# One product and a square root for the norm's variance, weight splits moved behind VectorE's, and w1 and w2 of three blocks in three rounded passes

## The reference, cut to what matters

```python
xn = _layernorm(x)                                    # (x - m) / sqrt(v + 1e-5), over 128 values
x = x + attn0(xn) + ffn0(xn)
# attn0: in_w, a causal convolution of 4 taps, silu, xp_w, a scan over time, out_w
# ffn0:  h = silu((xn @ w1.T) * s1) * ((xn @ w2.T) * s2)      # 128 -> 512
#        h = gelu((h @ h1.T) * t1); h = gelu((h @ h2.T) * t2)  # 512 -> 512, twice
#        h @ w3.T * s3                                        # 512 -> 128
xn = _layernorm(x)
x = x + ttt(xn) + moe(xn)                             # layer 1: test-time training, mixture of experts
```

## Time and profile before

| | |
|---|---|
| median of 3 runs | 646.53 us (643.77 to 649.48) |
| the profiled execution, its own time | 649.79 us |
| its span, first to last instruction | 647.9 us |
| TensorE busy / VectorE / ScalarE / GpSimd | 590.3 / 474.3 / 300.1 / 287.5 us |
| mean granted TensorE clock | 0.955 of 2.4 GHz |

### The profile page before, as it was taken

The page is one execution under the profiler, slowest core; times in us unless marked ns, Lnnn a source line. Parts: engine busy times, 40 slices in busy tenths (PEclk is TensorE's granted clock), DMA queues, the critical chain, the costliest instruction groups (busy, mean ns, idle before and its releaser), DMA issues.

```text
span 647.9 us, 14287 instructions
## 1 busy us (share of the span) xinstructions
PE 590.3 (91%) x5563; PEld 431.5 (67%) x5563; DVE 474.3 (73%) x898; ACT 300.1 (46%) x582; POOL 287.5 (44%) x267
## 2 busy tenths in 40 slices
PE   3979999999998997997999999899999989988786
PEld 1456676575566654665678778778778768766575
DVE  0593385794696287989769869787869769779892
ACT  1434245544545451633556355556356365344202
POOL 1970000025255353547431855962745945526411
PEclk9999899999897998997999999999999789999789
DMA  7999100001000100002625206234214322100401
GB/s 244 310 298 300 44 1 1 16 6 46 1 0 29 39 16 23 18 2 82 195 69 150 88 8 192 77 101 147 72 35 121 111 91 74 42 19 15 131 17 50
DMA packets 37890, 53.15 MB, mean 82 GB/s; under 512 B 10168, under 2 KB 23120, under 8 KB 37440
## 3 DMA queue, kind: packets, MB, share of 16 engines
q1 hardware_dynamic: 35552, 47.56, 24.4%
q0 software_dynamic: 2272, 4.69, 2.2%
HBM read 36.33 MB, written 15.90 MB: 81 GB/s over the span
## 4 chain that ended last, share of the span: by engine, by line
PE 64%; DVE 24%; POOL 6%; issue 4%; ACT 2%; DMA 0%; POOLq 0%; SPq 0%; ACTq 0%; DVEq 0%
PE ps L984 9%; PE ps L1087 7%; PE ps L841 7%; PE ps L1050 5%; PE ps L1058 4%; PE ps L1153 4%; PE ps L1095 4%; PE ps L847 3%; PE ps L1010 3%; POOL small L693 3%; PE ps L1137 3%; DVE small L1861 2%; PE ps L955 2%; PE ps L901 2%; PE ps L904 2%
## 5 line engine op out<-in xcount | busy, mean ns | idle before, releaser
L693 POOL TENSOR_TENSOR small<-small 128x8 f32<-128x8 f32 x32 | 53.4, 1680 | 108.7 <-DVE small L1799 108.6
L776 POOL TENSOR_TENSOR small<-small 128x8 f32<-128x8 f32 x32 | 51.9, 1635 | 37.8 <-DVE small L1791 37.8
L634 POOL TENSOR_TENSOR small<-small 128x4 f32<-128x4 f32 x8 | 8.7, 1093 | 116.7 <-DVE small L1554 116.7
L737 POOL DMA_INDIRECT ys_dram<-ybuf,slot_row x39 | 51.7, 1324 | 12.9 <-issue 8.6
L1407 ACT ACTIVATE sq<-ps 128x512 f32<-128x512 f32 x32 | 19.1, 597 | 72.0 <-PE ps L1087 72.0
L1439 ACT ACTIVATE work<-ps,b1t 128x128 f32<-128x128 f32 x156 | 44.5, 368 | 15.8 <-PE ps L1050 14.9
L1137 PE MATMUL ps<-grad,l 64*64 64x64 f32 x1024 | 33.0, 231 | 11.6 <-DVE grad L1876 10.8
L1398 ACT ACTIVATE x_query<-ps 128x512 f32<-128x512 f32 x32 | 17.5, 595 | 54.6 <-PE ps L1010 54.6
L1137 PEld LDWEIGHTS ps<-grad,l 64*64 64x64 f32 x1024 | 31.0, 144 | 16.0 <-issue 13.3
L1095 PE MATMUL ps<-grad,mats 64*64 64x512 f32 x224 | 35.7, 682 | 5.7 <-DVE sq L1805 3.4
L841 PE MATMUL ps<-act_parts,h_parts 128*128 128x512 f32 x128 | 37.4, 447 | 3.8 <-DVE act_parts L1721 3.8
(11 more groups left out here) (255 smaller groups left out, 1535.3 us busy)
## 6 DMA issues: line engine op xcount, KB each, us to landing
wtile<-in_mw SPq DMA_DIRECT2D x48, 256.0 KB, 3.4
xs_dram<-ybuf SPq DMA_DIRECT2D x1, 8840.0 KB, 37.8
got<-in_mw SPq DMA_DIRECT2D x30, 256.0 KB
xg<-xs_dram SPq DMA_DIRECT2D x40, 65.0 KB
got<-ys_dram SPq DMA_DIRECT2D x4, 512.0 KB, 5.4
x_sb<-in_xT SPq DMA_DIRECT2D x4, 256.0 KB, 4.8
acc<-in_h SPq DMA_DIRECT2D x1, 1024.0 KB, 6.6
got<-in_h SPq DMA_DIRECT2D x1, 1024.0 KB, 8.7
```

The costliest lines, as they stand in the source:

```text
L693: pool.tensor_tensor(small[:, 240 + 8 * p:248 + 8 * p], small[:, 224 + 8 * p:232 + 8 * p], small[:, 384:392], ALU.pow).then_inc(q_r.sem, 1)
L737: pool.indirect_dma_start(ys_dram, bass.IndirectOffsetOnAxis(ap=slot_row[:, k:k + 1], axis=0), ybuf[:, k // 4 % 2, k % 4], None).then_inc( ...
L776: pool.tensor_tensor(small[:, 16 + 8 * p:24 + 8 * p], small[:, 8 * p:8 * p + 8], small[:, 384:392], ALU.pow).then_inc(z_r.sem, 1)
```

## The change

- **Norm.** The four narrow products are one product of the mean matrix with all 512 columns of squares, so that every partition gets every variance at once. ScalarE takes the root with the epsilon as bias, VectorE takes the reciprocal of the 128x512 result in place and multiplies. `deviations`, `spreads`, `diagonals` and `spread_over` are gone. For `ahead_of[0]`, root, reciprocal and multiplication stand earlier: ScalarE's root ahead of the `h1` gelus, VectorE's part between the two halves of the convolution.
- **w1 and w2.** In blocks 1 to 3 each of the 8 float32 products is three rounded passes. VectorE splits the normalised block into `xn_hi` and `xn_lo` after the rests of `h1`'s activations, GpSimd splits `w1` and `w2`.
- **GpSimd.** The splits of `w1` and `w2` and the four operations for layer 1 wait until VectorE has split block 1 (`x_lo`). The splits of `wk` and `wq` wait until VectorE's last rest of block 3 (`a_gl`), and `split_tokens(0)`, which stood among block 2's work, follows them.

```diff
             def squares_mean(turn, i):
...
-                for j in range(NB // P):
-                    mm = pe.matmul(to[:, j:j + 1], lsq[:, j * P:(j + 1) * P], mats[:, M_MEAN * P:M_MEAN * P + 1],
-                                   start=True, stop=True)
-                mm.then_inc(ln_var, 1)
-            def spread_over(turn, i):
-                pe.wait_ge(ln_dg, norm_no[turn, i] + 1)
-                pe.matmul(slot_bank("norm", turn, i), mat(M_MEAN), lsq, start=True, stop=True).then_inc(ln_bc, 1)
+                pe.matmul(to, mat(M_MEAN), lsq, start=True, stop=True).then_inc(ln_var, 1)
...
+                if i:
+                    pe.wait_ge(x_lo, i)
+                    pe.wait_ge(h_sp, 4 * KC + 4)
                 for m in range(KC):
-                    pe.matmul(open_slot("w1", i, m), w1[:, m * P:(m + 1) * P], xn[:, blk(i)], start=True, stop=True)
-                    pe.matmul(open_slot("w2", i, m), w2[:, m * P:(m + 1) * P], xn[:, blk(i)],
-                              start=True, stop=True).then_inc(a_w12.sem, 1)
+                    for kind, w, parts in (("w1", w1, xb_s), ("w2", w2, xb_t)):
+                        to = open_slot(kind, i, m)
+                        at = slice(m * P, (m + 1) * P)
+                        if i:
+                            pe.matmul(to, parts[:, 0, at], xn_hi[:, :], start=True, stop=False)
+                            pe.matmul(to, parts[:, 1, at], xn_hi[:, :], start=False, stop=False)
+                            mm = pe.matmul(to, parts[:, 0, at], xn_lo[:, :], start=False, stop=True)
+                        else:
+                            mm = pe.matmul(to, w[:, at], xn[:, blk(i)], start=True, stop=True)
+                    mm.then_inc(a_w12.sem, 1)
...
             def spread_in(turn, i):
-                act.wait_ge(ln_bc, n + 1)
-                act.activation(lsq, slot_bank("norm", turn, i), ACT.Copy).then_inc(ln_rb, 1)
+                act.wait_ge(ln_var, n + 1)
+                act.activation(lsq, slot_bank("norm", turn, i), ACT.Sqrt, bias=eps_ln[:, 0:1]).then_inc(ln_rb, 1)
...
             def normalised(turn, i):
+                dve.reciprocal(lsq, lsq).then_inc(ln_iv, 1)
+                dve.wait_ge(ln_iv, n + 1)
...
-                        if m == 1 and t == 1:
-                            diagonals(*ahead_of[0])
                     if m == 0:
-                        deviations(*ahead_of[0])
+                        normalised(*ahead_of[0])
...
-                normalised(*ahead_of[0])
+                if i < NBLK - 1:
+                    dve.wait_ge(ln_out.sem, ln_out.at(norm_no[ahead_of[0]], 1))
+                    dve.tensor_copy(xn_hi[:, :], xn[:, blk(i + 1)]).then_inc(x_hi, 1)
+                    dve.wait_ge(x_hi, i + 1)
+                    tt(xn_lo[:, :], xn[:, blk(i + 1)], xn_hi[:, :], ALU.subtract).then_inc(x_lo, 1)
...
+            pool.wait_ge(x_lo, 1)
+            for w, to in ((w1, xb_s), (w2, xb_t)):
+                pool.tensor_copy(to[:, 0], w).then_inc(h_sp, 1)
+                parts[0] += 2
+                pool.wait_ge(h_sp, parts[0] - 1)
+                pool.tensor_tensor(to[:, 1], w, to[:, 0], ALU.subtract).then_inc(h_sp, 1)
             step(pool.tensor_tensor(wv_f, wk_f, wv_f, ALU.subtract))
...
             pool.wait_ge(ln_out.sem, ln_out.at(norm_no[1, 0], 1))
-            split_tokens(0)
-            spreads(1, 2)
             pool.wait_ge(a_h1.sem, a_h1.at(NBLK - 1, KC))
+            pool.wait_ge(a_gl.sem, a_gl.at(NBLK - 1, KC))
             split(wk, wk_f)
             split(wq, wq_f)
+            pool.wait_ge(a_w12.sem, a_w12.at(NBLK - 1, KC))
+            split_tokens(0)
```

More of the change, by code:

```diff
@@ L143, in build @@
         xb_t = sb("xb_t", [P, 2, NB], F32R)
+        with ExitStack() as first_layer:
+            xn_hi = first_layer.enter_context(nc.sbuf_tensor("xn_hi", [P, NB], F32R))
         x_less = sb("x_less", [P, NB])
+        xn_lo = sb("xn_lo", [P, NB], F32R)
         work = sb("work", [P, 8192])
@@ L260, in build @@
         eps_set, pads_set = sem("eps_set"), sem("pads_set")
-        ln_centred, ln_sq, ln_var, ln_sd, ln_rs, ln_dg, ln_bc, ln_rb = (
-            sem(n) for n in ("ln_centred", "ln_sq", "ln_var", "ln_sd", "ln_rs", "ln_dg", "ln_bc", "ln_rb"))
+        ln_centred, ln_sq, ln_var, ln_rb, ln_iv = (
+            sem(n) for n in ("ln_centred", "ln_sq", "ln_var", "ln_rb", "ln_iv"))
         ln_out = signal("ln_out", 1)
@@ L274, in build @@
         a_gh, a_gl = signal("a_gh", KC), signal("a_gl", KC)
-        h_sp = sem("h_sp")
+        h_sp, x_hi, x_lo = sem("h_sp"), sem("x_hi"), sem("x_lo")
         a_h1 = signal("a_h1", KC)
@@ L629, in _ @@
             pool.memset(zeros, 0.0).then_inc(zeroed, 1)
[L631 to L634, removed]
             parts = [0]
@@ L893, in _ @@
             squares_mean(0, 0)
-            spread_over(0, 0)
             for i in range(NBLK):
@@ L923, in _ @@
                 by_lo(to, h1_hi, a_h1.sem)
-                spread_over(*ahead_of[0])
                 to = [open_slot("h2", i, m) for m in range(KC)]
@@ L956, in _ @@
                 mm.then_inc(a_w3.sem, 1)
-                if len(ahead_of) == 2:
-                    spread_over(*ahead_of[1])
                 to = open_slot("out", i, 0)
@@ L1184, in _ @@
             key_bias(0, 0)
-            spread_over(1, NBLK - 1)
             keys_through(0, 0)
@@ L1303, in _ @@
             act.wait_ge(eps_set, 3)
-            act.activation(small[:, 100:102], eps_ln, ACT.Square)
+            act.activation(small[:, 100:102], eps_ln, ACT.Sqrt)
             squared(0, 0)
@@ L1328, in _ @@
                     gates_in(i - 2)
+                spread_in(*ahead_of[0])
                 for m in range(KC):
@@ L1333, in _ @@
                                    scale=col("h1_s", m)).then_inc(a_g1.sem, 1)
-                spread_in(*ahead_of[0])
                 for m in range(DC):
@@ L1550, in _ @@
             tt, ts, stt = dve.tensor_tensor, dve.tensor_scalar, dve.scalar_tensor_tensor
-            def deviations(turn, i):
-                dve.wait_ge(ln_var, norm_no[turn, i] + 1)
-                ts(dev[:, 0:4], slot_bank("norm", turn, i)[:, 0:4], LN_EPS, None, ALU.add).then_inc(ln_sd, 1)
-            def diagonals(turn, i):
-                dve.wait_ge(ln_rs, norm_no[turn, i] + 1)
-                for j in range(NB // P):
-                    ins = ts(lsq[:, j * P:(j + 1) * P], mat(M_IDENT), dev[:, j:j + 1], float(P), ALU.mult, ALU.mult)
-                ins.then_inc(ln_dg, 1)
             def normalised(turn, i):
-                dve.wait_ge(ln_rb, norm_no[turn, i] + 1)
+                n = norm_no[turn, i]
+                dve.wait_ge(ln_rb, n + 1)
+                dve.reciprocal(lsq, lsq).then_inc(ln_iv, 1)
+                dve.wait_ge(ln_iv, n + 1)
                 o = xn[:, blk(i)]
@@ L1686, in _ @@
             dve.wait_ge(ld_x, 32)
-            deviations(0, 0)
-            diagonals(0, 0)
             normalised(0, 0)
@@ L1745, in _ @@
                                            ALU.mult, ALU.add).then_inc(a_y.sem, 1)
-                if len(ahead_of) == 2:
-                    deviations(*ahead_of[1])
-                    diagonals(*ahead_of[1])
                 if i == NBLK - 1:
@@ L1768, in _ @@
                         tt(wt[:, 1, half], slot_bank("wt", 0, p), wt[:, 0, half], ALU.subtract).then_inc(w_t, 1)
-            deviations(1, NBLK - 1)
-            diagonals(1, NBLK - 1)
             normalised(1, NBLK - 1)
```

7 lines of the change are left out of this document (1 added, 6 removed).

## The result

The changed kernel takes **657.18 us** in the median of four executions (655.96 to 659.45), the kernel before 646.35 in the runs beside it (643.77 to 649.48): a ratio of **1.017, 95% interval 1.0115 to 1.0224**, slower. The prediction said 650.9, within 633 to 658, and gave "slower" 28%. The measured time lies inside the whole range but outside the forecast's own range, 644 to 655: the range holds because its upper end was kept for a reciprocal of 4.4 us, which did not occur. In the medians the change costs 10.8 us, and the sum gave 4.4. Comparisons leave out executions that stand over 1.5% above the fastest of the same kernel.

What follows compares the result with a forecast made beforehand. Stages were taken as bound by TensorE unless a row shows it waiting. Terms -0.7 - 2.0 - 0.5 + 1.5 + 1.1 + 1.45 + 3.5 = +4.4 us, on a median of 646.5, gave 650.9 us, range 633 to 658.

Steps and rivals of the forecast that it cites:

- forecast's own range: Range of the main forecast, 644 to 655 us, given 47%; the whole range took in a fast and a slow reciprocal.
- the reciprocal: VectorE's 128x512 reciprocal in each norm: 3.4 us, with 0.7 and 4.4 kept as the ends.
- Six places on the path: The reciprocal lies on TensorE's way at the start, in blocks 0 to 3 and at the last norm.
- The first rival: The 128x512 reciprocal is an ordinary instruction of 0.7 us, giving 634.5 us; chance 25%.
- second rival: The reciprocal takes over 8 ns for each element, 4.4 us, giving 657.5 us; chance 16%.
- where the waits stand: TensorE waits about 1.7, 2.7, 4.6 and 4.6 us before h2 in blocks 0 to 3; GpSimd delays block 0's scan.
- Rival three: GpSimd's long row blocks nobody: scan instructions pass beside it, giving 641.4 us; chance 8%.
- TensorE should keep its clock: Block 0: GpSimd's operations no longer lie beside h2, so its 16 passes take 3.80 us instead of 5.49.
- two losses of 1.7 outside what is hidden: Waits of 4.6, 4.6 and 5.5 us in blocks 2 and 3 cost two unhidden clock losses, +3.5 us.
- clock term: The sum's part for low clock behind TensorE's new waits: +3.5 us, between 0 and 5.1.
- 0.7 us gained at the start: Start to in_w: one product, root, reciprocal and multiplication end at 16.3 where in_w started at 17.04, -0.7 us.
- block 0's -2.0: Block 0: h2 starts earlier, but the scan, held by GpSimd, ends at 62.0; -2.0 us with 2.7 of waiting.

Runs made afterwards that it cites:

- e1: Changed kernel without the 128x512 reciprocal in each of the eight norms: mean 634.1 us of the lower pair of executions.
- e2: Changed kernel with every reciprocal of a norm done twice in a row: mean 676.2 us of the lower pair of executions.
- e4: Changed kernel with products nobody reads put into TensorE's waits before h2 in blocks 0 to 3: 660.4 us, against 660.6 by the ratio for the changed kernel.
- e5: Changed kernel with GpSimd's work back where it stood before, new norm and rounded passes kept: 664.4 us, ratio 1.0278 to the kernel before.
- e11: Kernel before with only GpSimd's work in the change's places, w1 and w2 still float32: 649.5 us, ratio 1.0062.
- e3: Changed kernel with the norm as before, rounded passes of w1 and w2 and GpSimd's new order kept: 655.9 us, ratio 1.006 to the kernel before.
- e8: e3 with GpSimd's four operations behind block 0's scan and the tokens' parts ahead of the wk and wq splits: 637.9 us, ratio 0.987 to the kernel before.
- e12: Kernel before with only the new norm, GpSimd's order and float32 w1 and w2 kept: 656.7 us, ratio 1.016.

## Why the prediction came out as it did

| up to | forecast, us against before | measured |
|---|---|---|
| `in_w` of block 0 | -0.7 | 16.56 - 17.04 = -0.5 |
| `h2` of block 0 | -3.0 | 42.97 - 46.14 = -3.2 |
| block 1 | -2.7 | 70.5 - 70.4 = +0.1 |
| block 2 | -3.2 | 115.3 - 114.2 = +1.1 |
| block 3 | -1.7, and 1.7 of clock: 0 | 166.5 - 162.3 = +4.2 |
| layer 1 | -0.6, and 3.5 of clock: +2.9 | 219.2 - 213.7 = +5.5 |
| gates of the last norm | +4.4 | 234.14 - 226.60 = +7.5 |

**Right: the reciprocal.** 3.35 us for 3.4. Six places on the path, in their sum shown by e1 and e2. The first rival (0.7 us) and the second (4.4) are both out. That the measured 657.2 falls on the second rival's 657.5 is chance. The Trainium skill ("VectorE: DVE Perf Modes", First, the fixed hardware budget) names a repeat count of 8; read as eight cycles it gave 4.3 us by estimate, and the row, 3346 ns, decides against that reading.

**Right: where the waits stand.** 2.34, 4.04 and 4.15 before `h2` for 2.7, 4.6 and 4.6; `out_w` behind the scan and GpSimd (62.49 for 62.0); the mask behind GpSimd, 45.8 us behind its block's `in_w` for 47.6. Two sizes are off: 3.48 us before block 0's `h2` for 1.7, since TensorE was ready at 39.5 and not at 41.4, and 2.44 before the mask for the 5.5 that 209.8 - 204.3 gives. Rival three, that GpSimd blocks nobody, is out by the rows of the scan.

**The step that failed: the clock.** "TensorE should keep its clock" in block 0, and "two losses of 1.7 outside what is hidden". With (1 - clock) x length the windows give 1.6 + 1.8 + 0 + 5.1 + 0 = 8.5 us lost before and 3.2 + 3.6 + 2.0 + 4.7 + 1.6 = 15.2 after: +6.7, where the forecast had 3.5 - 1.7 = +1.8. Block 0's `h2` still waited 3.48 us and still took 5.5, which the wait before `out_w` hid; the products behind its scan took 3.58 instead of 2.05, which nothing hid; block 1 had a slow stretch (5.37) that was given none; w3 behind the mask another.

How much of it reached the end can be read stage by stage. Against the forecast without its clock term the stages are longer by 2.8 (up to block 1), 1.5, 1.7, 0.1 and 0.6 us, 6.7 in all, where 3.5 had been set aside for the clock. Of the first 2.8 only some 1.6 are clock. 0.5 is the scan, and 0.7 is an error of the sum: the 0.7 us gained at the start were added to block 0's -2.0, though VectorE, which bounds that block, ended the first half of its convolution no earlier than before (35.66 for 35.75). So 5.5 us of the 6.7 are at most clock, 2 more than the term.

That the low clock follows from the waits is shown only in part. e4 removes it by filling them. But equal waits are not followed by equal clocks: 2.34 us and then 5.37 for 16 passes in the changed kernel, 2.35 and then 3.92 in e5; 2.44 us and then w3 in 5.38, in e2 2.12 and then 3.68. The part of layer 1 that the change doesn't touch took 413.6 us in one profiled execution and 411.2 in the other. What sets the clock from one execution to the next stays open.

**Also off: the step to the median.** From profile to profile the change cost 655.96 - 649.79 = 6.2 us, 1.8 above the sum. The other 4.5 are the executions: the one of before stood 3.3 above its median, the one of after 1.2 below. I took 3.3 off as if both stood alike.

**What the prediction did not ask.** It priced GpSimd's move by its waits and missed that its worth depends on the norm: alone it costs 0.6% (e11), with the new norm and the passes it saves 7 us (e5 to the change), and in other places, with the old norm, it is 1.9% or 12 us better than where it was put (e3 to e8).

## What to carry to other kernels

Before a slow instruction goes into an engine's stream, look for that engine's own gap: moved from the middle of the convolution to before the scan, where VectorE had waited 6.77 us for ScalarE, the same reciprocals of 3.35 us took the kernel from 1.7% slower to 1.35% faster. A part that "costs" in the profile (GpSimd's order) must be tried with the others as they will be, since its sign changed with them. And time saved on an engine that waits later in the same stage is not saved; price each gain from the wait that ends last in its stage.

## What the runs showed of the hardware

- VectorE's reciprocal goes by the element: 3346 ns for 128x512 against 178 for 128x4, 6.2 ns for each further element, and it kept 3.35 us where GpSimd worked beside it for some 2 us of it, on 128x512 (e5, 35.87 to 39.22) and on 128x1024 (e12, the fences below). Others stretched beside 128x1024: three taps, which read two tensors, took 8.20 us for 2.33 (e5), a 16x512 one 2.63 for 0.68, and also the one behind the product in e12, which reads one tensor and a column, 2.48 for 0.48. First VectorE in e12, then GpSimd:

```profile
35.46 3.35 DVE L1542 RECIPROCAL got<-got 128x512 f32<-128x512 f32 x1
...
39.45 2.48 DVE L1686 TENSOR_SCALAR work<-work,cols 128x512 f32<-128x512 f32 x1
```

```profile
36.83 2.40 POOL L668 TENSOR_TENSOR wst<-sq,wst 128x1024 f32<-128x1024 f32 x1 [4.03 <-DMA wtile<-in_wkT]
```

- Twelve scatters occupy GpSimd for 17.5 us in e3 (203.37 to 220.86), and the power of 1.06 us behind them has TensorE waiting 3.04 us.
- ScalarE's switch of functions before the last root cost one table load directly behind the key copy and directly ahead of the root:

```profile
226.05 1.29 ACT L1378 ACTIVATE work<-ps 128x512 f32<-128x512 f32 x2 [0.96 <-PE ps L983]
227.35 1.28 ACT L1291 ACT_TABLE_LOAD   x1
228.65 0.69 ACT L1291 ACTIVATE got<-ps,small 128x512 f32<-128x512 f32 x1
```

The Trainium skill ("ScalarE: Activation LUTs", What ACT_TABLE_LOAD costs) adds a drain of about 1.38 us; here 0.01 us lies ahead of the load and 0.02 behind it.
- Products that nobody reads, put into a wait, kept TensorE at 2.4 GHz behind it (e4, 42.61 to 46.40: granted clock 1.00, 16 passes in 3.86 us for 5.50), and the low clock then came in the next stretch (61.79 to 71.85: 0.62).
